# The front of a two-layer recurrent kernel: bias splitting moved between GpSimd's first powers, the second chunk's logits moved up, and ten multiplications of x on TensorE ahead of the first rows

## What is computed

```python
x = L0_attn_x
xn = _layernorm(x, axis=-1)
s = _L0_attn_ref(xn, ...)            # rmsnorm, five projections, gated linear scan, output projection, residual
g = _silu(_L0_ffn_ref(xn, ...))      # router: logits = xn @ Wr + br, softmax, top 1 of 4 experts
x = x + s * g
xn = _layernorm(x, axis=-1)
s = _L1_attn_ref(xn, ...)            # selective state space layer, 16 states
g = _silu(_L1_ffn_ref(xn, ...))      # binarized 256x256 weight
x = x + s * g
```

## Time and profile before

| | |
|---|---|
| median of 3 runs (lowest to highest) | 1465.36 us (1464.84 to 1466.21) |
| the profiled execution's own time | 1466.01 us |
| its span | 1464.2 us |
| TensorE (PE), VectorE (DVE) busy in the span | 1402.5 us (96%), 1026.9 us (70%) |
| ScalarE (ACT), GpSimd (POOL) busy | 892.9 us (61%), 915.8 us (63%) |

### The profile page before, as it was taken

One profiled execution on the slowest core, in us unless ns is written; L12 is line 12 of the kernel. 1 busy time (PEld: TensorE's weight loads), 2 busy tenths in 40 slices (PEclk: granted clock), 3 DMA queues, 4 the chain that ended last, 5 costly groups with the idle time before them and its releaser, 6 DMA issues.

```text
span 1464.2 us, 24214 instructions
## 1 busy us (share of the span) xinstructions
PE 1402.5 (96%) x9104; PEld 1125.7 (77%) x9104; DVE 1026.9 (70%) x1373; ACT 892.9 (61%) x1465; POOL 915.8 (63%) x463
## 2 busy tenths in 40 slices
PE   5999999999999999679899999999999999999998
PEld 3454469999999999347677877878778778788887
DVE  7655542232332323478899898998998998998997
ACT  3211121111111111289989989999899899899993
POOL 4422211222222222139989989989989989899895
PEclk9999999999999999899999999999999999999999
DMA  9921136666766763110121021210211211201211
GB/s 305 393 81 49 58 115 241 255 258 232 265 252 248 272 239 149 41 59 30 45 73 45 31 86 45 73 58 32 81 48 45 87 44 45 73 30 45 87 57 46
DMA packets 53283, 172.70 MB, mean 118 GB/s; under 512 B 6063, under 2 KB 32303, under 8 KB 48310
## 3 DMA queue, kind: packets, MB, share of 16 engines
q1 hardware_dynamic: 46038, 150.22, 29.2%
q0 software_dynamic: 7136, 21.01, 4.3%
HBM read 141.78 MB, written 31.00 MB: 118 GB/s over the span
## 4 chain that ended last, share of the span: by engine, by line
PE 79%; DVE 10%; ACT 5%; issue 4%; DMA 1%; POOL 1%; SPq 0%; DVEq 0%; POOLq 0%; ACTq 0%
PE bank L1481 17%; PE bank L1662 11%; PE bank L1679 11%; PE bank L1427 9%; PE bank L1494 8%; DVE hst L1321 4%; PE bank L1553 4%; PE bank L1583 3%; PE bank L1619 3%; PE bank L1591 2%; PE bank L1546 2%; ACT dA L857 2%; PE bank L1456 1%; PE bank L1564 1%; DVE bank L1198 1%
## 5 line engine op out<-in xcount | busy, mean ns | idle before, releaser
L1321 DVE TENSOR_TENSOR_SCAN hst<-dA,carry,bank 128x512 f32<-128x512 f32 x512 | 633.3, 1269 | 54.3 <-PE bank L1662 49.7
L667 POOL TENSOR_TENSOR hst<-hst,c_bc 128x2048 f32<-128x2048 f32 x127 | 578.2, 4557 | 23.2 <-DVE hst L1321 8.5
L857 ACT ACTIVATE dA<-delta,negA 128x512 f32<-128x512 f32 x512 | 358.0, 714 | 2.4 <-DVE hst L1321 1.9
L1662 PEld LDWEIGHTS bank<-ident,dbuT 128*128 128x128 f32 x2048 | 243.2, 141 | 136.9 <-issue 73.9
L1662 PE MATMUL bank<-ident,dbuT 128*128 128x128 f32 x2048 | 312.8, 276 | 17.1 <-DVE hst L1321 11.9
L1679 PE MATMUL bank<-ident,hst 128*128 128x128 f32 x2016 | 291.1, 273 | 0.0
L846 ACT ACTIVATE dbuT<-duT,bT 128x512 f32<-128x512 f32 x386 | 274.5, 712 | 1.5 <-PE bank L1662 1.5
L1481 PEld LDWEIGHTS bank<-f_sb,w_gu 128*128 128x128 f32 x2240 | 255.5, 192 | 2.7 <-ACT f_sb L729 1.0
L1481 PE MATMUL bank<-f_sb,w_gu 128*128 128x128 f32 x2240 | 256.0, 275 | 0.7 <-ACT f_sb L729 0.7
L1679 PEld LDWEIGHTS bank<-ident,hst 128*128 128x128 f32 x2016 | 234.1, 141 | 0.0
L610 POOL TENSOR_TENSOR x_sb<-x_sb,neg_half 128x1 f32<-128x1 f32 x35 | 23.1, 659 | 261.4 <-DVE x_sb L1144 261.4
(11 more groups left out here) (207 smaller groups left out, 1711.6 us busy)
## 6 DMA issues: line engine op xcount, KB each, us to landing
w_gu<-in_w_gu SPq DMA_DIRECT2D x35, 2048.0 KB, 7.3
c_bc<-c_rows SPq DMA_DIRECT2D x64, 512.0 KB, 3.7
sorted_x<-sg_a SPq DMA_DIRECT2D x12, 387.0 KB, 11.1
x_ld<-x_xn SPq DMA_DIRECT2D x9, 512.0 KB, 5.2
x_sb<-sorted_x SPq DMA_DIRECT2D x35, 129.0 KB, 7.2
x_sb<-in_x SPq DMA_DIRECT2D x8, 512.0 KB, 7.9
w_d<-in_w_d SPq DMA_DIRECT2D x1, 4096.0 KB, 21.3
x_mix<-x_sb SPq DMA_DIRECT2D x1, 4096.0 KB, 32.1
```

The source lines that it names most:

```text
L667: pool.tensor_tensor(h[:], h[:], c, ALU.mult).then_inc(hc_ready, 1)
L857: act.activation(dA[:, at % DA_BUFS, :], delta[q % B][:, d, :], ACT.Exp, scale=negA[:, d, n:n + 1]).then_inc(dA_ready, 1)
L1321: v.tensor_tensor_scan(h[:, d, :], dA[:, at % DA_BUFS, :], bank[4 + u % 2][:], carry1[q % B][:, n, d:d + 1], ALU.mult, ALU.add).then_inc(s ...
L1662: ins = pe.transpose(bank[4 + u % 2][:, i * P:(i + 1) * P], dbuT[(DS * q + n) % DBU_BUFS][:, i, d * P:(d + 1) * P], ident[:])
```

## The change

Three things are done. `split_biases` becomes a function of k that holds one cast, one multiplication and one addition; it is called behind GpSimd's second power (k = 0) and behind its third (k = 1). The two last casts stay behind `split_output`. On TensorE `logits(1, 1)` stands directly behind `logits(0, 0)`, and the loop leaves it out. Ahead of all that TensorE multiplies a piece of x ten times by x into bank 7, one product for each tile whose sums VectorE has taken (`tile_stats`, at most 8), and nobody reads the result.

```diff
+WARM = 10
...
-            def split_biases():
+            biases, taken = bias_f[:, 0:3 * D].rearrange("p (b d) -> p b d", d=D), bias_f[:, 3 * D:]
+
+            def split_biases(k):
                 pool.wait_ge(ld_small, 16 * 4)
-                biases, taken = bias_f[:, 0:3 * D].rearrange("p (b d) -> p b d", d=D), bias_f[:, 3 * D:]
-                for k in range(PARTS - 1):
-                    part, less = (bias_b[0:PARTS, :, half, :] for half in range(2))
-                    then(pool.tensor_copy(part, biases))
-                    then(pool.tensor_tensor(less, part, taken[:, k:k + 1].unsqueeze(2).broadcast_to([PARTS, PARTS, D]),
-                                            ALU.mult))
-                    then(pool.tensor_tensor(biases, biases, less, ALU.add))
-                for half in range(2):
-                    pool.tensor_copy(bias_b[0:PARTS, :, half, :], biases).then_inc(split_ready, 1)
+                part, less = (bias_b[0:PARTS, :, half, :] for half in range(2))
+                then(pool.tensor_copy(part, biases))
+                then(pool.tensor_tensor(less, part, taken[:, k:k + 1].unsqueeze(2).broadcast_to([PARTS, PARTS, D]),
+                                        ALU.mult))
+                then(pool.tensor_tensor(biases, biases, less, ALU.add))
 
             quarter = TILES // 4
             for k in range(4):
                 part = slice(k * quarter, (k + 1) * quarter)
                 pool.wait_ge(stats_ready, k + 1)
                 pool.tensor_tensor(rr0[:, part], tmp0[:, 1, part], neg_half[:, part], ALU.pow).then_inc(rr_ready, 1)
+                if 1 <= k < PARTS:
+                    split_biases(k - 1)
             pool.tensor_tensor(rstd0[:], tmp0[:, 0, :], neg_half[:], ALU.pow).then_inc(rstd_ready, 1)
             pool.wait_ge(xr_ready, TPC * CHUNKS)
             split_output()
-            split_biases()
+            for half in range(2):
+                pool.tensor_copy(bias_b[0:PARTS, :, half, :], biases).then_inc(split_ready, 1)
...
+            pe.wait_ge(ld_x[0], 16)
+            for i in range(WARM):
+                pe.wait_ge(tile_stats, min(i + 1, 2 * TPC))
+                pe.matmul(bank[7][:, 0:D], x_sb[:, 0, 0:P], x_sb[:, 0, :], start=True, stop=True)
             pe.wait_ge(ld_first, 32)
...
             logits(0, 0)
+            logits(1, 1)
             for c in range(2, CHUNKS):
                 turn_inputs(c, c % 2)
-                logits(c - 1, (c - 1) % 2)
+                if c > 2:
+                    logits(c - 1, (c - 1) % 2)
                 turn_logits(c - 2, c % 2)
```

## The result

| | before | with the change |
|---|---|---|
| median (lowest to highest), 10 executions each | 1464.88 us (1463.66 to 1466.21) | 1469.09 us (1468.25 to 1469.84) |
| ratio with its 95% interval | | 1.0031 (1.0023 to 1.0040) |
| the profiled execution's own time, its span | 1466.01, 1464.2 us | 1469.64, 1467.8 us |

The change makes the kernel 4.2 us slower, more than the 2.9 us that a measurement can tell from none. The forecast was +3.5 us, 1468.9.

A forecast was written before the change was run, and what follows sets the result against it. VectorE was taken to set the front's pace until 26.52 us, then TensorE's backlog. +5.3 for blocked scaled rows and -1.8 for the routing chain gave +3.5 us, forecast 1468.9, range 1467.5 to 1471.5.

The forecast's parts named there:

- Biases out of the chain: VectorE's routing chain, free of GpSimd's bias splitting, runs faster; the ranks move from 49.09 to 47.30: -1.8 us.
- Scaled rows blocked: VectorE's scaled rows beside the bias splitting wait for GpSimd in two windows, 2.7 us each: +5.3 us.
- The slack of TensorE at chunk 6: Chunk 6's rows are ready 0.6 us before its transposes; a little of the windows' 5.4 us is hidden, leaving +5.3.
- Early logits: Second chunk's logits moved before chunk 2 on TensorE only lengthen its idle time before chunk 4: 0 us.
- Ten products: Ten products of x at TensorE's start speed the first sixteen transposes by some 1.6 us, hidden behind VectorE: 0 us.
- Rival C: TensorE idles about 4.8 us before chunk 4, its clock falls: up to 1472; about a quarter of the forecast's 0.65.
- A: Only VectorE's two-input operations wait for GpSimd: 0.85 late, ranks -1.8, net -0.9 us, 1464.4; chance 0.27.
- B: Bias splitting and VectorE don't collide, as data lands late or pieces fall beside sums: -1.8 us, 1463.5; chance 0.08.
- near 38: Sign of a right forecast: TensorE's transposes of chunk 6 stand near 38 us in the trace.

The follow-up runs named there:

- e2: Kernel before, with only GpSimd's bias splitting moved behind the second and third power, TensorE's program unchanged: +3.6 us, ratio 1.0025.
- e10: Changed kernel, with scaled rows written in the form with an accumulator output (scaling by rr0 missing): +2.0 us against the kernel before, ratio 1.0014.
- e3: Changed kernel, with the second half of the bias splitting back behind the output weight: +1.1 us against the kernel before, ratio 1.0007.
- e4: Changed kernel, with six more unread products of x on TensorE before chunk 2 and before chunk 4: +2.7 us against the kernel before, ratio 1.0020.
- e8: Kernel before, with only the second chunk's logits moved up on TensorE: -0.1 us, ratio 1.0000.
- e1: Changed kernel, with the biases back behind split_output, so only TensorE's two parts stay: +0.7 us against the kernel before, ratio 1.0007.
- e7: Kernel before, with three GpSimd fills of bias_b behind the second and the third power, biases unmoved: +5.0 us, ratio 1.0035.
- e9: Kernel before, with bias_f loaded by ScalarE's queue and the first half of the bias splitting before the first power: -1.0 us, ratio 0.9990.
- e5: Kernel before, with GpSimd's second half of the bias splitting held until the one-hot exists: +1.2 us, ratio 1.0006.
- e6: Kernel before, with bias_f loaded by SyncE's queue behind x's first piece and the splitting's first half before the first power: 0.0 us, ratio 0.9998.

## Why the prediction was right, and where it was off

1. **Biases out of the chain, -1.8.** Right: R - T fell by 1.95 in the change and by 1.96 in e2. The chain's operations ran at 0.28 to 0.29, and TensorE went from its projections to the ranks without a wait (54.23, where 50.69 + 3.70 with its modelled end gives 54.39), as forecast from the earlier trace rows.
2. **Scaled rows blocked, +5.3.** Right in mechanism, and 0.25 too high: 2.53 a window for 2.7. The step that decided was reading L960's rate from the earlier trace rows; e10 shows that it was the rate, and e2 and e3 that the cost follows GpSimd's work. The Trainium skill (SBUF — State Buffer, the practical consequences under who interferes with whom) says that `tensor_scalar` in a two-port mode contends with GpSimd and that the form which also writes out its accumulator does not; both halves agree with the traces here, 3.89 for 1.37 us and 0.53 either way. The slack of TensorE at chunk 6 that was to swallow 0.1 didn't show: e2 and e4 pass on the 5.05 whole.
3. **Early logits, 0.** Right by itself (e8, T 0.00 and R 0.01). With late rows it is one of the two parts behind the 2.82 of the next point.
4. **Ten products, 0.** This step failed. It asked only whether the ten could delay TensorE or help it. What they did was to put it further ahead of VectorE, with nothing to do there: counted from the first scaled row, e1 is through with the second chunk's logits at 7.34 us and e8, without the ten, at 9.33, and e1's T is 1.67 later without any collision. In the change T is 2.82 later than in e2, which has the same late rows but before's TensorE program, and e4 gives that back. Which of the two TensorE parts it takes when the rows are late wasn't separated. With rows in time the early logits alone don't do it (e8); whether the ten products alone would isn't shown.
5. **Rival C, a quarter of the forecast's chance.** It came true, in another shape: not one idle time of 4.8 us before chunk 4 but two of about 3, the first of them before chunk 2. Its price, 1.6 to 3.2, holds 2.83. The estimate of one long gap had TensorE work at full speed up to chunk 4. But the first window makes chunk 2's rows late already: TensorE waits there in e2 too (3.91), without either TensorE part. The clock fell behind that wait, chunk 3's transposes and chunk 2's logits took 1.64 longer, and that filled most of what the estimate had as idle before chunk 4.
6. **Rivals A and B** are out: e2 and e3 show single windows of 2.53, where A had 0.75 and B nothing.

Forecast plus C would be +3.5 + 2.8 = 6.3, and R moved by 5.93; the time moved by 4.2 (3.4 to 5.9, so its interval just reaches what R shows). In most of the other kernels R and the time agree within 0.6 us: e2 3.10 and 3.6, e3 1.31 and 1.1, e4 3.12 and 2.7, e7 5.22 and 5.0, e8 0.0 and -0.1, e9 -1.6 and -1.0, e10 1.42 and 2.0. e1 is further off (1.74 and 0.7); in e5 and e6 the difference lies outside R, in the scans and in the wait for x. Between layer 1's first transposes, 5.00 later than before, and the span's end, 3.6 later, the change's profiled execution gets 1.4 us back: TensorE's waits for the scans there are shorter (10.4 us in all, 11.9 before). That doesn't take the change: in e8, whose front is before's to 0.01, these waits are 10.4 too, and from layer 1's first transposes to the end it takes 863.7 us, where before takes 865.0 and the change 863.6. What is left between R and the medians stays open.

That the forecast median lies 0.2 us from the measured one is luck. The forecast stood on a median of 1465.36 for the kernel before, which was 1464.88 beside the change: +3.5 was forecast and +4.2 measured. And in the front the forecast's two terms make 5.05 - 1.95 = +3.1, to which the clock added 2.83 that the likeliest case didn't hold.

**What the signs said.** L962's mean over `xn_st` is 0.720, single rows reach 1.78, the round is 9.10, the one-hot 0.29, the ranks without a wait: all as named. The clock's part was named only as C: chunk 6's transposes stand at 39.95 for "near 38", and the clock is at 0.50 between 30 and 37.

## What to carry to other kernels

Before work is moved to an idle GpSimd, look at what VectorE does beside it, and read from its durations per column whether that operation uses both ways into SBUF: with two SBUF inputs, or one at the double rate, it stood still here for whole GpSimd casts, multiplications and additions; sums, reductions and the accumulator form didn't, and GpSimd's powers held nothing up. A collision that is moved finds the next such operation (e5), so look for a stretch with none of them (e9). And making a fast engine earlier than its supplier has a price when its clock can fall: the time won is spent idle, and what comes behind may run at half speed. That costs only where the slow work isn't over before the next rows come (the change against e2).

## What the runs showed of the hardware

- A GpSimd fill without inputs blocks a double-rate `TENSOR_SCALAR` as an addition does (e7: 3.92 and 3.96 for 1.37). A GpSimd power blocks nothing: in the change it ran from 35.16 to 40.58, and beside it the scaled rows of the last round took their normal 1.38, as in the earlier trace rows.
- Small scans with two inputs, 128 x 32, are held just as well: four took 4.17 for 1.01 us, the longest 1.67 for 0.23 (e5). The longest scaled row took 1.78 for 0.40 (the change). Both lost about 1.4 us, near the length of GpSimd's multiplication (1.46), so the factor is larger for the smaller operation.
- TensorE's granted clock fell to 1.2 GHz after an idle time of 1.97 us that followed one of 0.67 (e1), in e10 after 1.21 and 0.41, and in every kernel with 2.68 or more before chunk 2 (the change 3.19, e2 3.91, e3 3.19, e7 2.68). The fall isn't tied to the idle time's end: in the change the clock was still at 1.00 when chunk 2's transposes began at 21.69, and fell in the stretch from 23 to 24. It held with 1.14 (the row at the end) and later 1.79 in the kernel before, with 0.69 (e8), with 1.72 (e4) and with 1.58 (e5). The length of one idle time alone doesn't tell these apart. Six products of x in each idle time were enough to hold it here (e4).
- At the start of TensorE's work the column of the granted clock can't be relied on: in the kernel before it reads 1.00 in every stretch from 13 to 17 us, where eight transposes take 1.94 us for the 1.09 that they take later.

```profile
19.95 1.10 PE L1370 MATMUL bank<-ident,xn_st 128*128 128x128 f32 x8 [1.14 <-DVE xn_st L960]
```
